# Set-up of a recurrent layer: three weight blocks move from VectorE to GpSimd

## What is computed

```python
xW = jnp.einsum('ntd,dg->ntg', x, Wx) + b
def step(carry, xw_t):
    prev_h, prev_c = carry
    a = xw_t + prev_h @ Wh                      # 4 * 512 columns
    i, f, o = (sigmoid(a[:, k * 512:(k + 1) * 512]) for k in range(3))
    g = jnp.tanh(a[:, 1536:])
    next_c = f * prev_c + i * g
    next_h = o * jnp.tanh(next_c)
    return (next_h, next_c), next_h
return x + hs                                   # hs: all next_h
```

## Time and profile before

| | us |
|---|---|
| median of 3 runs (lowest to highest) | 1855.11 (1855.08 to 1855.83) |
| profiled execution, time | 1856.47 |
| its span, first to last instruction | 1854.4 |
| VectorE busy | 1713.2 (92%) |
| TensorE busy | 1674.3 (90%) |
| ScalarE busy | 1011.4 (55%) |
| GpSimd busy | 539.3 (29%) |

### The profile page before, as it was taken

One profiled execution on the slowest core, in us unless ns is written; L12 is line 12 of the kernel. 1 busy time (PEld: TensorE's weight loads), 2 busy tenths in 40 slices (PEclk: granted clock), 3 DMA queues, 4 the chain that ended last, 5 costly groups with the idle time before them and its releaser, 6 DMA issues.

```text
span 1854.4 us, 106048 instructions
## 1 busy us (share of the span) xinstructions
PE 1674.3 (90%) x45116; PEld 1065.3 (57%) x45116; DVE 1713.2 (92%) x9739; ACT 1011.4 (55%) x3985; POOL 539.3 (29%) x1560
## 2 busy tenths in 40 slices
PE   1999999999999999999999999999999999999997
PEld 0555555555555555555555555555555555555555
DVE  8999999999999999999999999999999999999998
ACT  4555555555555555555555555555555555555554
POOL 0222223322332222233223332222232233322222
PEclk9999999999999999999999999999999999999999
DMA  5000000000000000000000000000000000000000
GB/s 210 15 26 21 21 23 23 21 21 26 21 21 26 21 21 21 26 21 21 26 21 21 26 21 21 21 27 21 21 26 21 21 24 24 21 21 27 18 12 14
DMA packets 39067, 49.03 MB, mean 26 GB/s; under 512 B 4416, under 2 KB 36160, under 8 KB 38592
## 3 DMA queue, kind: packets, MB, share of 16 engines
q1 hardware_dynamic: 37152, 37.77, 6.3%
q10 hardware_dynamic: 1440, 4.49, 0.6%
HBM read 25.46 MB, written 16.78 MB: 23 GB/s over the span
## 4 chain that ended last, share of the span: by engine, by line
DVE 70%; PE 19%; ACT 7%; issue 3%; DMA 1%; ACTq 0%; DVEq 0%
DVE turned L510 22%; DVE mailbox L514 13%; PE acc L311 12%; DVE products L523 11%; ACT gates L260 7%; PE acc L317 7%; DVE h_halves L538 5%; DVE h_halves L547 3%; DVE gates L532 3%; DVE x_halves L493 3%; DVE out_ring L575 3%; DVE h_feat L542 3%; DVE x_tops L586 2%; DVE mailbox L528 2%; DMA wh<-in_wh 1%
## 5 line engine op out<-in xcount | busy, mean ns | idle before, releaser
L311 PE MATMUL acc<-wh_low,h_halves 128*32 128x256 f16 x16384 | 719.4, 274 | 135.6 <-DVE h_halves L538 133.8
L317 PE MATMUL acc<-wh_high,h_halves 128*32 128x256 f16 x16384 | 722.3, 275 | 0.0
L303 PE MATMUL x_acc<-wx_high,x_halves 128*32 128x512 f16 x8192 | 621.5, 380 | 1.1 <-ACT x_acc L234 1.1
L311 PEld LDWEIGHTS acc<-wh_low,h_halves 128*32 128x32 f16 x16384 | 390.5, 96 | 395.3 <-DVE h_halves L538 383.8
L260 ACT ACTIVATE gates<-mailbox 128x96 f32<-128x96 f32 x1024 | 257.1, 251 | 634.1 <-DVE mailbox L514 634.1
L510 DVE STREAM_TRANSPOSE turned<-acc 128x256 f32<-128x256 f32 x1024 | 458.9, 448 | 57.2 <-PE acc L317 51.4
L194 POOL TENSOR_SCALAR o_gate<-gates,scales 128x32 f32<-128x32 f32 x1024 | 372.7, 364 | 419.4 <-ACT gates L265 419.4
L186 POOL TENSOR_TENSOR o_preact<-turned 128x32 f32<-128x32 f32 x512 | 163.4, 319 | 892.0 <-DVE turned L510 892.0
L317 PEld LDWEIGHTS acc<-wh_high,h_halves 128*32 128x32 f16 x16384 | 343.6, 96 | 113.8
L303 PE MATMUL x_acc<-wx_low,x_halves 128*32 128x512 f16 x4096 | 399.2, 380 | 0.0
L237 ACT ACTIVATE acc<-x_acc,step_mask 128x512 f32<-128x512 f32 x512 | 334.8, 654 | 4.7 <-PE x_acc L303 4.7
(11 more groups left out here) (67 smaller groups left out, 696.5 us busy)
## 6 DMA issues: line engine op xcount, KB each, us to landing
out<-out_ring SPq DMA_DIRECT2D x128, 128.0 KB, 2.1
x_ring<-in_x SPq DMA_DIRECT2D x120, 128.0 KB, 2.9
wx<-in_wx ACTq DMA_DIRECT2D x4, 512.0 KB, 8.1
wx<-in_wx SPq DMA_DIRECT2D x4, 512.0 KB, 8.1
wh<-in_wh SPq DMA_DIRECT2D x4, 512.0 KB, 16.7
wh<-in_wh ACTq DMA_DIRECT2D x4, 512.0 KB, 17.1
x_ring<-in_x SPq DMA_DIRECT2D x2, 512.0 KB, 16.7
b_rows<-in_b ACTq DMA_DIRECT2D x1, 256.0 KB, 21.4
```

The lines of the kernel that those rows point to most:

```text
L303: last = pe.matmul(x_acc[pair % 2][32 * j:32 * j + 32], x_halves[:, pair % (CHUNK // 2), c, half], w[:, c].rearrange("p (n q) g -> p q n g ...
L311: pe.matmul(acc[par][32 * j:32 * j + 32, n, 0:GL], h_halves[1 - par][:, c, 0:2], w_low["wh"][:, c, n * Q + j], start=False, stop=False, sk ...
L317: last = pe.matmul(acc[par][32 * j:32 * j + 32, n, 0:GL], h_halves[1 - par][:, c, 1:3], w_high["wh"][:, c, n * Q + j], start=False, stop=c ...
```

## The change

GpSimd's program gets the low halves of blocks 0, 1 and 2 of Wx ahead of the loop: it scales the fp32 block in place in two instructions, once ScalarE has read it for the high half, and subtracts the high half in a third. VectorE keeps block 3 alone, and comes to the scale of Wh directly behind the scale of x. The sums of Wh move from a bank of `acc` to `mailbox[0]`, as `acc` may be opened by then. ScalarE halves the bias, and places the first bias ahead of blocks 1 to 3 of the high half of Wh. TensorE opens its banks behind the first high half, and takes Wx blocks in the order 0, 1, 3, 2, each behind its own semaphore `wx_low_done[c]`.

```diff
-        wh_sums = acc[0][:, 1, 0:4]
+        wh_sums = mailbox[0][:, 256:260]
...
-        wx_low_done = sem("wx_low_done")
+        wx_scaled = sem("wx_scaled")
+        wx_low_done = [sem(f"wx_low_done{c}") for c in range(C)]
...
+            pool.wait_ge(wx_scale_ready, 1)
+            for c in range(C - 1):
+                pool.wait_ge(wx_high_done, c + 1)
+                for cols, scale in ((slice(0, 64), wx_scale), (slice(64, GL), half_scale[:, 0:1])):
+                    pool.tensor_scalar(w32["wx"][:, c, :, cols], w32["wx"][:, c, :, cols], scale, None, ALU.mult)\
+                        .then_inc(wx_scaled, 1)
+                pool.wait_ge(wx_scaled, 2 * (c + 1))
+                pool.tensor_tensor(w_low["wx"][:, c], w32["wx"][:, c], w_high["wx"][:, c], ALU.subtract)\
+                    .then_inc(wx_low_done[c], 1)
...
+            act.wait_ge(b_loaded, 16)
+            act.activation(b_rows[:, :, 64:GL], b_rows[:, :, 64:GL], ACT.Copy, scale=0.5).then_inc(b_ready, 1)
             act.wait_ge(wh_scale_ready, 1)
             high_of_w("wh", 1, 0, wh_high_done)
             act.wait_ge(x_loaded[0], 16)
             act.wait_ge(x_scale_ready, 1)
             high_of_x(0, 0)
-            high_of_w("wh", 1, 1, wh_high_done)
-            high_of_x(0, 1)
-            high_of_w("wh", 1, 2, wh_high_done)
-            high_of_w("wh", 1, 3, wh_high_done)
             act.reg_load(rescale[0], inverses[0][0:1, 3:4])
             act.reg_load(b_scale[0], scales[0][0:1, 3:4].bitcast(I32))
...
             act.wait_ge(b_ready, 1)
             act.wait_ge(acc_opened, 2 * NG + 2)
             place_bias(0)
+            high_of_w("wh", 1, 1, wh_high_done)
+            high_of_w("wh", 1, 2, wh_high_done)
+            high_of_w("wh", 1, 3, wh_high_done)
+            high_of_x(0, 1)
             place_bias(1)
...
-            pe.wait_ge(wx_low_done, C)
+            pe.wait_ge(wx_high_done, 1)
             pe.wait_ge(zeroed, 6)
...
-            input_part(0, (0, 1, 2, 3)).then_inc(x_summed, 1)
+            for c in (0, 1, 3, 2):
+                pe.wait_ge(wx_high_done, c + 1)
+                pe.wait_ge(wx_low_done[c], 1)
+                summed = input_part(0, (c,))
+            summed.then_inc(x_summed, 1)
...
-            low_of_w("wx", 0, 0, wx_high_done, wx_low_done)
             dve.wait_ge(sums_ready, 2)
             scale_of(wh_sums, 1, 3)
             dve.tensor_scalar(half_scale[:, 1:2], wh_scale, 0.5, None, ALU.mult).then_inc(wh_scale_ready, 1)
-            low_of_w("wx", 0, 1, wx_high_done, wx_low_done)
...
-            low_of_w("wx", 0, 2, wx_high_done, wx_low_done)
-            low_of_w("wx", 0, 3, wx_high_done, wx_low_done)
+            low_of_w("wx", 0, 3, wx_high_done, wx_low_done[3])
...
-            dve.wait_ge(b_loaded, 16)
-            dve.tensor_scalar(b_rows[:, :, 64:GL], b_rows[:, :, 64:GL], 0.5, None, ALU.mult).then_inc(b_ready, 1)
```

More of the change, by code:

```diff
@@ L220, in _, with place_bias, fill @@
             b_scale = [act.alloc_register(f"b_scale{p}") for p in range(2)]
+            def place_bias(pair):
+                act.activation(x_acc[pair % 2][:], b_rows[:], ACT.Copy, scale=b_scale[2 * pair // CHUNK % 2]).then_inc(bias_placed, 1)
+            def fill(t):
+                act.activation(acc[t % 2][:, :, 0:GL], x_acc[t // 2 % 2][:], ACT.Copy, scale=step_mask[:, t % 2:t % 2 + 1])\
+                    .then_inc(acc_filled, 1)
+            act.wait_ge(b_loaded, 16)
+            act.activation(b_rows[:, :, 64:GL], b_rows[:, :, 64:GL], ACT.Copy, scale=0.5).then_inc(b_ready, 1)
             act.wait_ge(wh_scale_ready, 1)
```

## The result

The changed kernel takes 1865.64 us (1865.14 to 1866.26, 6 runs) against 1855.28 us of the kernel before (6 runs): 10.4 us slower, a ratio of 1.0056 with a 95% interval of 1.0044 to 1.0068. That lies outside the forecast range, above its upper end. The profiled execution has a span of 1864.3 us in place of 1854.4.

The account below looks back on a forecast made before the run. VectorE's set-up chain was taken to set the first transpose: 44.0 undisturbed plus 8.7 of waiting on GpSimd gives 52.7, 1.5 later than before. That made the median 1856.6 us, range 1847.8 to 1860.8.

Parts of the forecast that it names:

- What bounds the kernel: Set-up before the time loop: VectorE's chain alone sets the first transpose at 51.18; the 512 steps behind stay 3.52 us each.
- what leaves VectorE: VectorE's set-up: three Wx blocks, 7.17, and the bias, at most 0.35, go; undisturbed, first transpose at 44.0, 7.2 earlier.
- ScalarE and TensorE: Set-up: halving the bias (done by 27.7) and opening banks (28.4 to 30.3) cost nothing; TensorE's tail 3.7 to 6.1.
- GpSimd's block: GpSimd's low half of one Wx block: scaling 2.1, subtraction 4.2, instructions 0.3, so 6.6; bounds 4.2 to 10.5.
- Do the engines disturb each other: Set-up from 30.6: GpSimd's remaining 9.4 holds up VectorE's two-input instructions, nearly all of it, bringing the transpose to 52.7.
- A: The forecast: GpSimd and VectorE take turns in set-up, first transpose at 52.7, 1.5 later; chance 0.47.
- the signs of A: Set-up trace: Wx block starts near 33.4 after a GpSimd subtraction; four Wh blocks at 2.39 each behind GpSimd's last instruction.
- its quick end, 46.2: Taking turns with a GpSimd block of only 4.2: first transpose at 44.0 + 2.2 = 46.2, 5.0 earlier.
- B: GpSimd and VectorE don't disturb each other in set-up: first transpose at 44.0 to 46.1, 7.2 to 5.1 earlier; chance 0.33.
- D: Little comes of it, as the two biases or the fill start the loop; shares the remaining chance of 0.03.
- C: GpSimd comes last, its block 2 ending late before TensorE's tail: transpose at 56.7 to 59.1, 5.5 to 7.9 later; chance 0.17.

Follow-up runs that it names:

- run 1: Changed kernel without GpSimd's part, VectorE making all four low halves of Wx: 1856.19 us against 1856.03 of the kernel before, ratio 1.0001.
- Run 3: Changed kernel with GpSimd making only block 0 of Wx and VectorE's two-element steps for the scale of Wh split into single elements: span 1851.7 us.
- Run 4: Changed kernel without GpSimd's scaling of its three blocks, subtractions alone, so part of the computation is left out: span 1850.4 us.
- run 5: Changed kernel with VectorE's small steps on two and four elements, the scales included, written as one-element steps: span 1863.0 us, first transpose at 59.85.
- run 7: Kernel before plus four GpSimd scalings of 2048 floats on private tiles, sharing only the scalar: span 1862.4 us, first transpose at 59.27.
- run 6: Changed kernel with one-element small steps and both steps splitting h0 moved behind the third Wh block: span 1864.1 us, first transpose at 60.86.
- run 9: Changed kernel with ScalarE scaling two Wx blocks, GpSimd only subtracting, VectorE keeping two, Wh scale in one-element steps: 1852.31 us against 1856.42 of kernel before, ratio 0.9979.

## Why the prediction was wrong

The forecast was a first transpose at 52.7, 1.5 later than before; it came at 61.5, 10.4 later. The direction was right, the size was not.

**What bounds the kernel, what leaves VectorE.** Both right. In run 1 the scale of x is there at 30.5 (30.6 forecast), and from the last Wx block to the transpose it is 13.5 (13.4 forecast). Run 3 gives 48.88 for one block moved, 2.3 earlier, a block being 2.39.

**ScalarE and TensorE.** Right that the bias and the opening are free.

**GpSimd's block.** This is the term that failed: 6.6 forecast, 9.8 measured. The subtraction's number was right (4.2 forecast, 4.07 measured), its reasoning was not: by passes per input a scaling would be the quicker of the two, and it is the slower. The scaling was taken at one pass of the fill, 2.1; it takes 5.7, 2.8 ns an element against the 1.03 of the earlier trace rows. I had named 10.5 as the upper end and wrote that I didn't believe in it; nothing in the rows spoke against it, and the truth was near it, though not by its terms (4.2 + 6.3 there, 5.7 + 4.1 measured). A write-only fill bounds a scaling from below and is no estimate of it. Run 4 prices the term: without it the transpose is at 47.59.

**Do the engines disturb each other.** Right in kind, and the weak evidence of the earlier trace rows was the right one to believe. By my sum for A with a block of 9.8 in place of 6.6 the transpose is at 44.0 + 3 x 9.8 - 10.4 - 0.7 = 62.3; measured 61.5. So the mis-sized block accounts for all of the miss of 8.8, and the sum as a whole was good to 0.8.

Two terms in it were still wrong, and that they nearly cancel is luck. I took off 0.7 for what VectorE gets done beside GpSimd; it got a Wx block and both steps on h0 done before 51.0, 2.9 of its work, so 2.2 more. And I let VectorE take nothing from GpSimd: GpSimd ends at 51.0 and not at 20.2 + 29.4 = 49.6, because it starts 0.2 late and its third scaling is held for about 1.1. With both, 62.3 - 2.2 + 1.4 = 61.5.

I also let VectorE's tiny steps run free. Those on two and four elements were held (1.66 and 3.79), so the scale of x came at 36.1 and not at 30.6, and the Wx block began at 39.9 and not at 33.4. That cost nothing of its own, as all of it lay in GpSimd's time; they used up turns that larger instructions could have had. The four Wh blocks did come behind GpSimd's last instruction, undisturbed, as the signs of A had it. (At its quick end, 46.2, the sum leaves out the 0.7.)

**Which VectorE instructions are held.** Held behind GpSimd's subtraction were a two-input step (4.07 on h0 at 47.01) and a one-input step on two elements (1.66); behind its scaling of 1536, one-input steps on four and on 64 elements (3.79, 4.15). Not held beside the subtraction were steps on one element (run 3) and a step on two elements that reads PSUM (0.16 at 28.47). Behind a scaling some were let in early: two-input ones 1.0 to 1.9 before its end (runs 5 and 7), and the one-input step on two elements at 30.36, which takes 0.62 (0.17 before) and ends at 30.98, while the scaling of 512 runs to 31.83.

The Trainium skill (SBUF — State Buffer, "Who interferes with whom") says that whichever engine starts first keeps the other out for the whole instruction, and that a one-input VectorE instruction in a two-port mode is kept out as well. The rows behind a subtraction agree; those behind a scaling agree only in part. The Trainium skill (VectorE: DVE Perf Modes, "Mode 2×_2P") gives as conditions of that mode that the operands lie in SBUF and that the outermost dimension of more than one element is even, or equal for source and destination. Run 3 agrees: two elements held, one element not, and one element has no such dimension; an odd number above one was not tried. The prediction quotes the two-input half of the rule and leaves out the other half, which bears on the scales.

The Trainium skill (GPSIMD Engine Reference, "Engine selection") says of GpSimd's elementwise operations that "1-input is roughly line-rate". The scaling here doesn't bear that out: 5.7 for 2048 elements, against 2.29 for a VectorE search over as many.

**Rivals.** B fell: VectorE was held. D fell too: what starts the loop after the change is VectorE's chain behind GpSimd. C wasn't what happened after the change (TensorE waited for x, not for block 2), but it is what runs 5 and 6 turned into, with a tail of 5.6 where it had named 3.7 to 6.1. It had been priced with the block of 6.6, so its 56.7 to 59.1 was too early as well.

## What to carry to other kernels

In a kernel like this one, work given to GpSimd isn't free just because GpSimd is idle. Count its time as time that VectorE's instructions with two SBUF inputs, and its one-input ones on two or more elements, may lose, and finish it while VectorE runs reductions or single elements: the last search of a Wh block took 2.29 beside GpSimd's scaling and subtraction, as it did in the kernel before. Measure the rate of each GpSimd operation that the change uses, as another operation's rate says little. An instruction held behind a long one costs the same however short it is (4.15 and 4.07 for 64 elements), so small steps on a critical chain should be of a form that isn't held, and should not be placed between long ones.

## What was not expected of the hardware

- GpSimd's scaling by a per-partition scalar takes 2.7 ns an element (4.15 us for 1536), its subtraction with two inputs, one of them fp16, 2.0 (4.07 for 2048): the operation with more inputs is the faster. Whether the scalar from memory or the fp32 output makes the difference was not tried; in place or not makes none (run 7).
- A VectorE instruction on two integers took 1.66 to 5.22 us behind a GpSimd instruction, those on one element 0.14 (run 3).
- A two-input VectorE instruction got in 1.0 us before the end of a scaling of 1536 elements and 1.9 before that of one of 2048, but only 0.2 before that of a subtraction (36.11, 4.56 in the changed kernel). The one-input steps on four and on 64 elements got in 0.2 before the end of a scaling. Why they differ was not looked into.
- TensorE's granted clock read 0.62 on average from 46.5 to 51.0 in run 9, so most of that stretch was at the lower of its two levels (1.2 of 2.4 GHz), behind a wait of 1.77 us, though it had run at full pace since 40.2. The same wait left the clock at 1.00 in run 1 and in the changed kernel, so the wait alone isn't the cause.
